# A graph kernel's distances come in as three bf16 rows and are spread over the partitions by PE

## The reference

```python
centers = jnp.linspace(R_MIN, R_MAX, IN_FEATS)           # 128 centers
bf = jnp.exp(coeff * (dist[:, None] - centers[None, :]) ** 2)
bf = ssp(bf @ W1 + b1)                                   # ssp(x) = softplus(x) - ln 2
bf = ssp(bf @ W2 + b2)
cut = jnp.where(dist < R_MAX, 0.5 * (jnp.cos(jnp.pi * dist / R_MAX) + 1.0), 0.0)
msg = h[src] * edge_feat * bf * cut[:, None]
agg = jax.ops.segment_prod(msg, dst, num_segments=n_nodes)
out = ssp(agg @ W3 + b3)
```

## Time and profile before

| | |
|---|---|
| median of 3 runs | 5082.86 us (5082.14 to 5086.49) |
| the profiled execution's own time | 5105.77 us, span 5104.0 us |
| busy, share of the span | PE 75%, DVE 62%, ACT 54%, POOL 37% |
| mean granted TensorE clock | 0.843 of full speed; 0.74 in the product stage |
| moved by DMA | 920 MB, 180 GB/s |

### The profile page before, as it was taken

How to read it: one execution, slowest core, us unless ns; L and a number is a source line. 1 busy time by engine, 2 the same in 40 slices (tenths; PEclk the granted TensorE clock), 3 DMA queues, 4 the chain that set the end, 5 groups by cost and what they waited for, 6 DMA issues and landing times. The chain is left out here.

```text
span 5104.0 us, 67054 instructions
## 1 busy us (share of the span) xinstructions
PE 3802.7 (75%) x22995; PEld 2424.4 (48%) x22995; DVE 3149.9 (62%) x5629; ACT 2755.1 (54%) x4313; POOL 1897.5 (37%) x1883
## 2 busy tenths in 40 slices
PE   3888887899999999999965665655656665566642
PEld 2777775444444444444434444443444444444432
DVE  7999997323232323232136777777777777777774
ACT  2666665222222222221017878877878787787863
POOL 4222001300100010001136666666666666666653
PEclk9888988999999999999976777777777677777775
DMA  3333333788877788877755555555555555555541
GB/s 108 132 136 129 126 130 133 227 240 248 243 232 240 244 246 242 255 242 235 224 145 157 171 166 172 167 171 170 168 164 173 172 172 165 166 169 167 172 141 54
DMA packets 641672, 920.47 MB, mean 180 GB/s; under 512 B 70098, under 2 KB 423239, under 8 KB 641431
## 3 DMA queue, kind: packets, MB, share of 16 engines
q1 hardware_dynamic: 550727, 782.65, 48.4%
q0 software_dynamic: 59936, 119.71, 8.8%
q10 hardware_dynamic: 30768, 15.26, 1.0%
HBM read 674.76 MB, written 242.59 MB: 180 GB/s over the span
## 5 line engine op out<-in xcount | busy, mean ns | idle before, releaser
L1306 POOL DMA_INDIRECT hgat<-x_rows,edge_src x1564 | 1497.4, 957 | 826.4 <-issue 453.4
L957 PE MATMUL bank<-gran,hp 128*128 128x490 bf16 x7056 | 1515.1, 373 | 26.6 <-DVE hp L1100 14.2
L957 PEld LDWEIGHTS bank<-gran,hp 128*128 128x128 bf16 x7056 | 678.0, 96 | 817.4 <-issue 29.6
L1373 PE MATMUL bank<-dist,v_sb 128*128 128x512 f32 x618 | 469.6, 849 | 737.9 <-issue 603.7
L1434 DVE TENSOR_SCALAR bank<-rows_e,edge_same,edge_first 128x128 f32<-128x128 f32 x1564 | 644.9, 412 | 121.7 <-DVE rows_e L1437 61.3
L810 POOL DMA_INDIRECT x_sb<-h_rows,last_i x147 | 139.2, 947 | 1540.6 <-DMA h_rows<-h_out 1473.8
L599 PEld LDWEIGHTS bank<-hi_hot,lo_hot 128*128 128x128 bf16 x7840 | 544.9, 155 | 223.3 <-issue 70.8
L599 PE MATMUL bank<-hi_hot,lo_hot 128*128 128x49 bf16 x7840 | 572.9, 219 | 101.4 <-DVE hi_hot L435 99.8
L540 ACT CAST stage<-bank 128x490 bf16<-128x490 f32 x784 | 451.9, 576 | 304.3 <-PE bank L599 304.3
L1386 PEld LDWEIGHTS bank<-v_sb,excess 128*128 128x128 f32 x2472 | 470.7, 262 | 281.8 <-issue 264.1
L1027 DVE TENSOR_SCALAR t<-bank,c_sb 128x512 f32<-128x512 f32 x82 | 61.5, 751 | 855.7 <-PE bank L932 848.3
(11 more groups left out here) (239 smaller groups left out, 4313.9 us busy)
## 6 DMA issues: line engine op xcount, KB each, us to landing
gran<-step_counts SPq DMA_DIRECT2D x336, 857.5 KB
dist<-weight_by_step SPq DMA_DIRECT2D x391, 256.0 KB
running_products<-rows_e SPq DMA_DIRECT2D x391, 256.0 KB
step_counts<-stage SPq DMA_DIRECT2D x112, 857.5 KB
ef<-in_edge_attr SPq DMA_DIRECT2D x391, 224.0 KB
hgat<-x_rows,edge_src POOLq DMA_INDIRECT x1564
kn<-keep_and_norm_of_steps SPq DMA_DIRECT2D x48, 490.0 KB
edge_filter_times_attr<-g_out SPq DMA_DIRECT2D x82, 256.0 KB, 3.6
```

The source lines that it names most:

```text
L957: last = nc.tensor.matmul(y, hp[:, 7 * g + i, part, :], gran[:, g, :, i * IS:(i + 1) * IS], start=first, stop=last_)
L1306: pool.indirect_dma_start(out=hgat[:, b % U, c, :], out_offset=None, in_=x1_d, in_offset=bass.IndirectOffsetOnAxis(ap=edge_src[:, b, c:c + ...
L1373: nc.tensor.matmul(ps1[f % R][:], v1_sb[:], dist[:, f % Q], start=True, stop=True).then_inc(s_z14, 1)
```

## The change

The preparation splits the distances into three bf16 parts that add up to the fp32 value, and stores them as three rows `wt3_d`. DVE makes three casts and two subtractions over `wt_t`, after the preparation's stores have landed; SP stores each part when it is ready, two transfers each, and the part ends when all have landed.

In the product stage `load_dist` brings three rows of 512 bf16 values (1 KB each) to three partitions, `dist3`. PE multiplies them by a [3, 128] block of ones (`spread_dist`), which puts the sum of the three parts on all 128 partitions of bank 7, and ACT's Square reads that bank and writes `dist`. SP's load now waits for the spread of the filter that used the buffer (`s_sp`); the spread waits for the load and for the Square of the filter before (one bank); the Square waits for the spread and for `z1` of the filter four back.

```diff
@@ preparation, sync and vector
+                    for n in range(3):
+                        sp.wait_ge(s_part, n + 1)
+                        sp.dma_start(wt3_d[n, 0:(KT - 1) * P * P].rearrange("(j k p) -> k j p", k=P, p=P),
+                                     wt_parts[n][:, 0:KT - 1, :]).then_inc(s_prep, 16)
+                        sp.dma_start(wt3_d[n, (KT - 1) * P * P:EP].rearrange("(k p) -> k p", p=P),
+                                     wt_parts[n][0:KR, KT - 1, :]).then_inc(s_prep, 16)
+                    sp.wait_ge(s_prep, 16 * 10)
...
+                    nc.vector.memset(wt_t[:, KT - 1, :], 0.0)
...
+                    dve.wait_ge(s_prep, 16 * 4)
+                    for n in range(3):
+                        nc.vector.tensor_copy(wt_parts[n][:], wt_t[:]).then_inc(s_part, 1)
+                        dve.wait_ge(s_part, n + 1)
+                        if n < 2:
+                            link(nc.vector.tensor_tensor(wt_t[:], wt_t[:], wt_parts[n][:], ALU.subtract))
@@ product stage, sync
-                                sp.wait_ge(s_z14, f - Q + 1)
-                            sp.dma_start(dist[:, f % Q], wt_row[:, b * BLK:(b + 1) * BLK].to_broadcast([P, BLK])
-                                         ).then_inc(s_di[f % Q], 16)
+                                sp.wait_ge(s_sp, f - Q + 1)
+                            sp.dma_start(dist3[:, f % Q], wt3_d[:, b * BLK:(b + 1) * BLK]).then_inc(s_di[f % Q], 16)
@@ scalar
-                            act.wait_ge(s_di[f % Q], 16 * (f // Q + 1))
-                            nc.scalar.activation(part, part, ACT.Square, bias=center[:]).then_inc(s_sq4, 1)
+                            act.wait_ge(s_sp, f + 1)
+                            if f >= Q:
+                                act.wait_ge(s_z14, f - Q + 1)
+                            nc.scalar.activation(part, spread[:], ACT.Square, bias=center[:]).then_inc(s_sq4, 1)
@@ tensor
+                    def spread_dist(f):
+                        if f < ND:
+                            pe.wait_ge(s_di[f % Q], 16 * (f // Q + 1))
+                            if f:
+                                pe.wait_ge(s_sq4, f)
+                            nc.tensor.matmul(spread[:], one_3[:], dist3[:, f % Q], start=True, stop=True).then_inc(s_sp, 1)
...
+                    pe.wait_ge(s_one3, 1)
+                    spread_dist(0)
+                    spread_dist(1)
                     z1(0)
                     pe.wait_ge(s_one, 1)
                     for n in range(ND + LAG):
+                        spread_dist(n + 2)
                         z1(n + 1)
                         z2(n - 1)
@@ vector
+                    nc.vector.memset(one_3[:], 1.0).then_inc(s_one3, 1)
```

More of the change, by code:

```diff
@@ L69, in gnn @@
     wt_d = scratch("weight_by_step", (EP,), F32)
+    wt3_d = scratch("weight_parts_by_step", (3, EP), BF16)
     pk_d = scratch("packed_edges", (EP,), I32)
@@ L130, in gnn @@
             wt_t = sbt("wt_t", [P, KT, P])
+            wt_parts = [sbt(f"wt_part{n}", [P, KT, P], BF16) for n in range(3)]
+            s_part = psem("s_weight_parts")
             half_pi = sbt("half_pi", [P, 1])
@@ L178, in _ @@
                                  ).then_inc(s_prep, 16)
-                    sp.wait_ge(s_prep, 16 * 4)
+                    for n in range(3):
[5 more added lines that the diff above has]
+                    sp.wait_ge(s_prep, 16 * 10)
                     sp.wait_ge(s_fd, 16 * 3)
@@ L1220, in gnn @@
             dist = sbt("dist4", [P, Q, BLK])
+            dist3 = sbt("dist3", [3, Q, BLK], BF16)
+            one_3 = sbt("one_3", [3, P], BF16)
+            spread = banks[7]
+            s_sp, s_one3 = sem("s_dist_spread"), sem("s_ones3")
             ef4 = sbt("ef4", [P, Q, BLK])
@@ L1242, in gnn @@
             g_rows = g_d.rearrange("b p e -> p b e")
-            wt_row = wt_d.rearrange("(a b) -> a b", a=1)
             run_rows = run_d[0:EP, :].rearrange("(p k) d -> p k d", k=EPP)
```

## The result

| | median, us | runs |
|---|---|---|
| before | 5082.5 | 4, from 5080.0 to 5086.5 |
| changed | 5109.4 | 4, from 5104.1 to 5112.2 |

The ratio is 1.0051, with a 95% interval of 1.0038 to 1.0065. The changed kernel's profiled execution took 5109.0 us (span 5106.2). That of the kernel before took 23 us more than its own median, so the two spans can't be set against each other; the ratio can.

A forecast was written before the change was run, and what follows sets the result against it. The prediction took the product stage to be bound by the rate at which completions are counted, one in 42.0 ns. It summed 5082.9 + 11.5 − 142.8 + 20 = 4971.6, so 4970 us, its own range 4920 to 5030.

The forecast's parts named there:

- completion writes −142.8: Product stage: loads of distances make 11 fewer completion writes a filter, 3399 in all at 42.0 ns, −142.8 us.
- Rival A: Product stage: completions aren't the limit, it keeps 5.92 us a block and only preparation counts, 5094 us; chance 0.13.
- D: Loads of distances: the remainder is written one by one, 309 more writes than before, 5107 us; chance 0.09.
- Preparation, +11.5: Preparation: three casts and two subtractions on DVE, then issue and landing of the last stores, +11.5 us.
- Data, 0: Product stage: 256 KB a filter become 3 KB, but DMA is busy 55% and no wait names these loads, 0.
- PE, ACT and SP, 0: Product stage: PE's spread fits its standing time, ACT's shorter Square is off the limit, SP's moved wait unpriced; 0.
- Give-back, +20: Product stage: with POOL's limit nearer, some of the time no completion is waiting; 1% of the stage, +20 us.
- B: ACT's Square: its new wait for PE's spread lengthens each stall by 1.37 us, 5202 us; chance 0.10.
- C: Product stage: signals come on time, stalls end and POOL binds at 5.0 us a block, 4734 us; chance 0.07.

The follow-up runs named there:

- e6: Changed kernel with one load of distances for four filters and one load of edge_attr where it fills 128 rows: 5122.9 us, 1.0050 of the kernel before.
- e7: Kernel before with two more small transfers for each filter, 16 rows of 32 bytes each, which nobody reads: 5102.0 us, ratio 1.0007.
- e8: Kernel before with one load of edge_attr in place of two where it fills 128 rows: 5097.1 us, 0.9994 of the kernel before.
- e4: Changed kernel with one load of distances for four filters: 4722.1 us, 1.0005 of the kernel before, which took 4717.8 there.
- first set: First of five sets of experiments, each on one chip; the kernel before took 4717.8 us in it.
- e1: Kernel before with the change's preparation alone, its three parts made and stored but not read: 4729.2 us, 1.0023 of the kernel before.
- e9: Kernel before with the change's preparation alone, repeated where the kernel before took 5106.4 us: 5118.5 us, ratio 1.0028.
- e17: Changed kernel without its preparation's casts and subtractions, the three rows stored early as zeros: 5096.2 us, 1.0027 of the kernel before.
- e5: Changed kernel once more, unaltered, beside the kernel before at 5099.3 us: 5122.1 us, ratio 1.0043.
- e18: Changed kernel again, unaltered, beside the kernel before at 5083.0 us: 5109.1 us, ratio 1.0051.
- e13: Kernel before with each gather fetching half rows, 256 B in place of 512 B, from the seventh block on: 5101.2 us, ratio 0.9999.
- e11: Kernel before with four plain loads of 128 rows by SP in place of POOL's four indexed gathers a block: 4660.7 us, ratio 0.9125.
- e12: Kernel before with a block's running product made over all four rows together, 3 DVE signals a block in place of 9: 5087.0 us, ratio 0.9957.
- e2: Kernel before with one load of edge_attr in place of two where it fills 128 rows: 4712.0 us, 0.9991 of the kernel before at 4717.8.
- the fourth: Fourth of five sets of experiments, each on one chip; the kernel before took 5101.8 us in it.
- fifth set: Last of five sets of experiments, each on one chip; the kernel before took 5083.0 us in it.

## Why the prediction was wrong

- **The step that failed** is the term "completion writes −142.8", and under it the reading that the stage "is bound by the rate at which completions are counted". Two rates, 20.5 small packets a microsecond here and 8.7 elsewhere, were taken for a cause. e6, e7 and e8 vary the completion writes from −20% to +21% for nothing, and the change itself made 13 fewer a filter without shortening the stage. The count under the term was near: 3 packets and one update for the remainder (e4: 156 updates for 39 loads), and the signal `s_sp`, in place of 16. It is the 42.0 ns a write that no run shows. The term measured about 0 in place of −142.8.
- **What stood in its place:** POOL's indexed gathers. With them, signals of PE and DVE come late, ACT runs out of work, and POOL, which itself waits for those signals, stands too. Leave one of four out and 413 us go; let SP bring the same number of bytes and 446 go; add a fifth and 531 come. The gathers alone are not enough, though: in the first set the same kernel has the same gathers and no stalls, so a second condition is at work that these runs don't name. That PE's signals are late was read rightly from the earlier trace rows, but in the stall shown above PE's own products are late as well. All four gathers of a block stand in the earlier trace rows with 1285 and 1.48 us each; nothing in the change touched them.
- **Rival A** was the outcome: the stage keeps its 5.92 us a block (1900 x 4 / 1290 = 5.89). It had 0.13 and gave 5094. D's 5107 is nearer, but its mechanism, 13 writes one by one, is excluded by e4's trace (4 updates a load of three rows, not 16).
- **Preparation, +11.5:** right; 10.0 in the profile, +11 us (e1), +14 (e9, interval 8 to 21).
- **Data, 0:** right. A fifth less data shortened no stall and not the stage.
- **PE, ACT and SP, 0:** too low together. e17 has +14 us (9 to 19) in the median, from the stage's part. The profiled stages, taken from ACT's first instruction in the stage to its first in the last part, don't show where: 2346, 2337 and 2348 us in before, e8 and e9, 2341, 2350 and 2342 in after, e5 and e18, and 2336 in e17. The Square's wait on a late PE signal, 1.37 us earlier in ACT's order than soft2's was, is a candidate that no run isolated. It stays open.
- **Give-back, +20:** void with the gain that it was taken from.
- **B** is excluded by 67 waits of the old length, **C** by their number. C's price, a stage at POOL's own 5.0 us a block, was right for the first set.

What in a gather holds up the other engines is not settled. Shown is that it goes with the number of indexed gathers, not with their bytes (e13), with as many bytes landing by plain loads (e11), with DVE's load (e12) or with the other transfers (e6, e7). A gather of fewer rows was not run, so gathers and gathered rows aren't told apart.

## What to carry to other kernels

When signals are late, list every engine that is at work without a gap in the microseconds before they come through, and remove each in turn in an experiment before a rate is made of any count. A high rate of something in the slow stage is only a correlation. Where indexed gathers by POOL bind, as here, count gathers of 128 rows: half the bytes of each were worth nothing.

## What the runs showed of the hardware

- The same kernel has two speeds, 4718 us (32 of the first set's 33 executions agree within 0.4%, one took 5971) and 5083 to 5106 us, by the set in which it ran. The profiled spans of before and e2 differ by 396 us: 355 in the product stage (1.26 us a gather without stalls, 1.48 with), 33 in the last part, which has its own stalls, and the rest ahead of them. The chip's number doesn't tell: 15 was the number in the first, the fourth and the fifth set. What decides is open.
- Where there are stalls, PE's products of one group, which wait for no signal of each other, start up to 2.8 us apart (timeline above). ACT goes on 14 us after the end that the trace gives for the product it waits for, and 28.7 us in the last part, beside 49 gathers without a pause.
- The stalls of the kernel before and after ended about 3 us after POOL's run of gathers had ended (3.05, 3.23 and 2.74 us in three of before, 3.07 in the one shown).
- An indexed gather of 128 rows takes 945 to 960 ns of POOL and 0.30 us between two, 1.25 us back to back.
- With a load of three rows in place of one to 128 partitions the packets of 4 bytes fell from 22587 to 18570, 13 for each of 309 filters, as three in place of sixteen do. With the load of three rows goes one semaphore update more, for the remainder (e4).
